# An attention and expert layer on one core: the order of far scores, maximum parts and the gated product within a pass of the loop

## The reference

```python
OFFSETS = sorted(set(range(0, 33)) | {48, 64, 96, 128, 192, 256, 384})
qkv = x @ Wqkv + bqkv                      # x: (16, 512, 256)
scores = stack([einsum('bhnd,bhnd->bhn', q, shift(k, d)) for d in OFFSETS]) * scale + pos_bias
alpha = softmax(where(invalid, -inf, scores))
flat = sum_i alpha[..., i] * shift(v, OFFSETS[i])
x = layernorm(x + (flat * sigmoid(x @ Wgate + bgate)) @ Wout + bout)
logits = relu(x @ rw1 + rb1) @ rw2 + rb2   # 8 experts, top 2, at most 1024 rows each
y = sum over the two experts of prob * (relu(row @ ew1 + eb1) @ ew2 + eb2)
out = layernorm(x + y)
```

## Time and profile before

| | |
|---|---|
| median of 3 timed runs | 2030.01 us (2027.12 to 2035.88) |
| the profiled execution's own time | 2021.59 us |
| its span, first to last instruction | 2019.9 us |
| PE busy | 1514.6 us, 75% |
| DVE busy | 988.9 us, 49% |
| ACT busy | 905.3 us, 45% |
| POOL busy | 705.7 us, 35% |
| mean granted TensorE clock | 0.796 of full speed |

### The profile page before, as it was taken

The page is one execution under the profiler, slowest core; times in us unless marked ns, Lnnn a source line. Parts: engine busy times, 40 slices in busy tenths (PEclk is TensorE's granted clock), DMA queues, the critical chain, the costliest instruction groups (busy, mean ns, idle before and its releaser), DMA issues. The chain is left out here.

```text
span 2019.9 us, 72320 instructions
## 1 busy us (share of the span) xinstructions
PE 1514.6 (75%) x31232; PEld 1005.1 (50%) x31232; DVE 988.9 (49%) x2117; ACT 905.3 (45%) x1544; POOL 705.7 (35%) x654
## 2 busy tenths in 40 slices
PE   0555787877787787878777887878765499999980
PEld 0234455555454555445554555545553266676660
DVE  4213445554545554555545544564644355555525
ACT  1231443635354453535444453544433365655626
POOL 4221313525333342525333342534323113323335
PEclk9765777868787777868787777868876699999995
DMA  2464624345352524335342524335220333443428
GB/s 77 74 171 156 134 56 98 98 77 125 80 114 79 108 73 93 97 70 115 85 98 75 105 70 88 91 78 110 58 57 14 108 105 85 95 114 85 74 28 337
DMA packets 220103, 194.55 MB, mean 96 GB/s; under 512 B 66847, under 2 KB 207151, under 8 KB 219648
## 3 DMA queue, kind: packets, MB, share of 16 engines
q1 hardware_dynamic: 204464, 175.11, 35.0%
q0 software_dynamic: 15360, 15.10, 4.7%
HBM read 98.07 MB, written 86.18 MB: 91 GB/s over the span
## 5 line engine op out<-in xcount | busy, mean ns | idle before, releaser
L394 POOL TENSOR_TENSOR p<-p 128x512 f16<-128x512 f32 x96 | 129.3, 1347 | 434.3 <-ACT p L794 434.2
L808 ACT COPY featT<-gp 128x1024 f16<-128x1024 f16 x96 | 93.3, 1031 | 329.3 <-PE gp L539 329.3
L394 DVE TENSOR_TENSOR p<-p 128x512 f16<-128x512 f32 x96 | 94.3, 982 | 288.0 <-ACT p L794 287.5
L546 PE MATMUL gp<-featT,wr 128*128 128x512 f16 x768 | 198.8, 416 | 24.2 <-DVE mT L957 15.4
L1105 POOL DMA_INDIRECT disp<-y,sidx x128 | 175.7, 1372 | 53.5 <-issue 37.9
L1359 POOL DMA_INDIRECT xln<-y,place x64 | 104.9, 1640 | 216.4 <-DVE y L1501 175.9
L1397 PE MATMUL up<-rowsT,w 128*128 128x512 f16 x768 | 170.1, 381 | 10.3 <-DVE w L1474 5.3
L1411 PE MATMUL dn<-w,h 128*128 128x256 f16 x1536 | 170.1, 273 | 0.0
L621 PE MATMUL o<-v_near,p 128*32 128x66 f16 x2048 | 134.6, 204 | 40.6 <-issue 29.1
L793 ACT ACTIVATE p<-st 128x512 f16<-128x512 f32 x192 | 116.6, 607 | 102.7 <-PE st L590 98.7
L1411 PEld LDWEIGHTS dn<-w,h 128*128 128x128 f16 x1536 | 149.7, 98 | 17.3
(11 more groups left out here) (176 smaller groups left out, 3138.1 us busy)
## 6 DMA issues: line engine op xcount, KB each, us to landing
qk_dram<-qk SPq DMA_DIRECT2D x64, 256.0 KB, 2.5
v_near<-vs SPq DMA_DIRECT2D x224, 66.0 KB
qs<-qk_dram SPq DMA_DIRECT2D x96, 128.0 KB, 4.6
ks<-qk_dram SPq DMA_DIRECT2D x96, 128.0 KB, 7.4
o_dram<-o_far SPq DMA_DIRECT2D x64, 136.0 KB, 5.7
o_back<-o_dram SPq DMA_DIRECT2D x16, 544.0 KB, 3.9
v_dram<-vs SPq DMA_DIRECT2D x16, 528.0 KB
v_far<-v_dram SPq DMA_DIRECT2D x64, 132.0 KB
```

The source lines that it names most:

```text
L394: engine.tensor_tensor(p16[:, b, 1, :], p32[:, b, :], p16[:, b, 0, :], ALU.subtract).then_inc(is_split, 1)
L546: last = nc.tensor.matmul(dst, lhs(a, c), rhs(b, c), start=(k == 0), stop=(k == len(todo) - 1))
L808: gp_done(nc.scalar.copy(featT[:, i, :, :].rearrange("f c t -> f (c t)"), bank[:, :].bitcast(F16)), n, stage, PART_OF_T[stage], i)
```

## The change

It changes three tables and nothing that an instruction computes.

- The second pair of far scores moves from slot 0 to slot 1, behind `qk0`, and its exponentials and subtractions move from slots 1 and 2 to slots 2 and 3.
- In slots 6 and 7 `near0` and `near1` stand ahead of `w` and `y`, where they stood behind.
- `near3`, `far0`, `far1` and `t` of the maximum stage move one slot later each. Slot 8 then holds `near2` alone; in slot 10 `far0` stands ahead of the router's transposes, in slot 11 `far1` ahead of `h0`, and `t` ahead of `h1` in slot 12.

```diff
@@ SLOTS_OF @@
-    6: [("outp", "w"), ("maxp", "near0")],
-    7: [("outp", "y"), ("maxp", "near1")], 8: [("maxp", "near2"), ("maxp", "near3")],
-    9: [("maxp", "far0")], 10: [("maxp", "far1"), ("rout", "t"), ("split", "x")],
-    11: [("maxp", "t"), ("rout", "h0"), ("rank", "s0"), ("rank", "s1")],
-    12: [("rout", "h1"), ("gate0", "den0"), ("gate0", "inv0")], 13: [("rout", "h2"), ("rank", "s2"), ("rank", "s3")], 14: [("rout", "h3")], 15: [("feat", "x")],
+    6: [("maxp", "near0"), ("outp", "w")], 7: [("maxp", "near1"), ("outp", "y")], 8: [("maxp", "near2")],
+    9: [("maxp", "near3")], 10: [("maxp", "far0"), ("rout", "t"), ("split", "x")],
+    11: [("maxp", "far1"), ("rout", "h0"), ("rank", "s0"), ("rank", "s1")],
+    12: [("maxp", "t"), ("rout", "h1"), ("gate0", "den0"), ("gate0", "inv0")], 13: [("rout", "h2"), ("rank", "s2"), ("rank", "s3")],
+    14: [("rout", "h3")], 15: [("feat", "x")],
@@ @@
-SCORES_AT = [-1, 0, 4, 7, 10, 12]
-EXP_AT = [0, 1, 5, 8, 11, 13]
-SPLIT_AT = [1, 2, 6, 9, 12, 14]
+SCORES_AT = [-1, 1, 4, 7, 10, 12]
+EXP_AT = [0, 2, 5, 8, 11, 13]
+SPLIT_AT = [1, 3, 6, 9, 12, 14]
```

## The result

The changed kernel took 2040.39 us (median of 19 runs, 2027.59 to 2050.77), the kernel before 2025.86 us (19 runs, 2019.50 to 2036.58) beside it. The ratio is 1.0065, with a 95% interval of 1.0049 to 1.0080. So it is slower by 0.65%, where I had forecast 1.7% faster, with slower at 0.13. The profiled execution took 2046.25 us, more than its median, and that of the kernel before (2021.59) took less than its own: the two traces lie 24.7 us apart, the medians 14.5.

A forecast was written before the change was run, and what follows sets the result against it. TensorE, busy 75% of the span, was taken as the bound through its waits. 29 us from 14 passes, 4 at the start and 2 for the clock gave 35: 1986.6 us profiled, 1995 median, range 1960 to 2036.

The forecast's parts named there:

- my sum: Gain per attention-loop pass: 0.5 us in one sample pass, 3.7 in the one before it, mean 2.1.
- Part 1: Second far scores behind first projection: direct gain 1.1 and 1.9 us a pass; ks lands 3.7 and 4.5 us earlier.
- Part 2: near0 ahead of the gated product: product ends 2.9 or 0.1 us later, near3 starts 11.6 us after it.
- Rival 2: Maximum stage: near2's reduction stays pinned to residual, stall before near0 costs 1 us more; 2026 to 2030 us, chance 0.15.
- Part 3: Maximum stage, one part to a slot, mT later: waits before near3, far0 and for mT go; 3.4 or 3.8 us gained.
- 19.7 remain: From near2's start to h1: 24.5 us, less three waits and near2 itself, leaves 19.7 us.
- pass B: Sample pass of the kernel before, one of two alternating kinds; x transposes end at 926.18; forecast gain 0.5 us.
- rival 4: Stall before near0 puts gated product and following work at 1.2 GHz, costing 14 to 20 us; 2009 to 2015, chance 0.13.
- my 35: Whole kernel: total forecast gain of 35 us, 29 from 14 passes, 4 at the start, 2 for the clock.
- Rival 3: Loads of ks land no earlier, so near0 holds TensorE; 2.0 us a pass more, 2058 us, chance 0.12.
- 17.1 and 19.1: Times in us from POOL's last projection subtraction to the last ks landing, in two sample passes, assumed unchanged.

The follow-up runs named there:

- 5: The whole change run again, against the kernel before, on a chip where that takes 1978 us: 1963.82 us, ratio 0.9915.
- 7: Far scores behind qk0, one part to a slot, near1 ahead of y, w still ahead of near0, against the kernel before: 1944.98 us, ratio 0.9830.
- 13: Only the far scores moved behind qk0, against the kernel before, on a chip where that takes 2028 us: 2001.54 us, ratio 0.9874.
- 16: Far scores behind qk0 and near1 ahead of y, maximum stage otherwise as before, against the kernel before: 1988.65 us, ratio 0.9785.
- 15: Far scores behind qk0, y a slot later on ACT and two on DVE, old maximum stage, against the kernel before: 1986.14 us, ratio 0.9765.
- `y` late: Far scores behind qk0, one part to a slot, y a slot later on ACT and two on DVE, against the kernel before: 1943.36 us, ratio 0.9815.
- 9: The changed kernel once more, against the kernel before, on a chip where that takes 2028 us: 2039.55 us, ratio 1.0048.
- 10: The changed kernel with row scatters two slots later (first half) and one later (second half); ratio against the kernel before: 2064.61 us, 1.0156.
- near1 first: Far scores behind qk0, one part to a slot, near1 ahead of y, y late on ACT and DVE, against the kernel before: 2016.82 us, ratio 0.9925.

## Why the prediction was wrong

The table holds mean us of a pass over twelve passes, worked out from TensorE's timeline. A stage counts from its start to the start of the next; the wait that stands before a stage is put to that stage, and the waits inside the maximum stage and for mT have rows of their own.

| stage | before | changed | before, chip without gaps | changed, same chip |
|---|---|---|---|---|
| transposes, projection, second far scores | 14.3 | 12.6 | 13.8 | 13.5 |
| near0 and gated product, with the 0.64 before the first near value product that went | 10.6 | 11.3 | 10.4 | 11.6 |
| waits for reductions inside the maximum stage | 5.7 | 5.6 | 5.7 | 5.6 |
| h0 | 3.9 | 4.7 | 3.6 | 4.6 |
| fourth near scores | 1.7 | 4.1 | 1.7 | 1.6 |
| wait for mT | 1.2 | 0 | 1.5 | 0 |
| h1 | 2.8 | 4.2 | 3.1 | 2.7 |
| third value product | 3.9 | 1.6 | 1.6 | 1.6 |
| h2 and h3 | 6.1 | 5.3 | 5.3 | 5.3 |
| fourth value product, first far scores | 4.1 | 6.1 | 4.3 | 4.4 |
| all other stages | 36.4 | 36.1 | 36.7 | 35.8 |
| pass | 90.5 | 91.7 | 87.6 | 86.7 |

The first three rows and that for mT are what my sum was made of. They gave 2.3 us a pass on the chip of the result, where I had 2.1. The rows from h0 on that I had left as they were cost 3.7.

**Part 1 was right.** The wait ahead of the projection is 1.21 in the pass shown, 1.9 in the mean where the two waits before made 3.5: a gain of 1.6, forecast 1.1 and 1.9. POOL's last subtraction of the projection came 12.8 us after the transposes of x (forecast 12 to 13). In three measurements on two chips the part by itself is worth 1.0 to 1.3%.

**Part 2 was nearly right, and its price was hidden in the sum.** near0 and the copies' wait together stand 4.9 us a pass (58.7 / 12) where 3.3 and 1.75 were forecast. near3 started 979.29 - 968.43 = 10.9 after the product's end; I had said 11.6. But what it buys is nothing: in the table the waits for reductions stay at 5.6, only moved for the most part onto near3 (4.87 in the pass shown). The reduction that it waits for stands behind the residual, as I had worked out. Rival 2 had no gain for this reason, but its own sign, near3 more than 13 us after the product, did not come. The two swaps of this part pull apart: near0 ahead of the product costs 0.9% (experiments 5 and 7), while near1 ahead of `y` alone, with near0 left behind the product, took 14.5 us of these waits off twelve passes (experiments 13 and 16, on two chips). Moving the residual instead took 29.6 (13 and 15). Neither has a wait on ks in those twelve passes.

**Part 3 was the step that failed:** "19.7 remain", that is, from near3's start to h1 without waits every duration was taken as in the kernel before. In the changed kernel it is 1002.69 - 979.29 = 23.4. The waits went as forecast: none for mT, and none before far0 (0.88 in pass B). But the fourth near scores took 5.03 (997.11 to 1002.14) in place of 1.7, and h0 4.5 (992.59 to 997.11) in place of 3.5; in the table it is 0.8 and 1.1 us longer a pass. Then h1, the first product behind the gaps, took 4.41 where I had 2.76. The sum from the fourth near scores to the first far scores is 18.5 before and 21.4 after, 2.8 more (table, its wait for mT apart); on the chip without gaps it is 15.9 and 15.5, 0.4 less. So in these stages the kernel before lost 2.6 us a pass to being on a chip with gaps, the changed one 5.8. All of its passes together differ by 2.9 and 5.0 between the two chips, so 0.3 and -0.8 us lie elsewhere.

These are the granted clocks of the changed kernel (length, busy per engine, PEclk, DMA share, GB/s), over the gaps and over h1 behind them, and then h1 in the kernel whose scatters come later and in the changed kernel on the chip without gaps:
```profile
997.11:1002.00 4.89, 2.60 (x71) 1.70 (x70) 1.07 (x2) 1.27 (x2) 3.30 (x4) 1.00 0.11 33
1002.69:1007.10 4.41, 4.41 (x17) 1.55 (x16) 4.23 (x4) 1.27 (x2) 0.00 (x0) 0.62 0.01 4
```
```profile
1016.52:1019.28 2.76, 2.76 (x16) 1.16 (x15) 2.62 (x3) 1.25 (x2) 0.00 (x0) 1.00 0.00 0
```
```profile
968.78:971.54 2.76, 2.76 (x16) 1.16 (x15) 2.62 (x3) 1.25 (x2) 2.46 (x2) 1.00 0.11 32
```
The clock was at its 2.4 GHz level (granted 1.00) in the gaps and at 1.2 GHz for part of h1 behind them (0.62 in the mean), so part of the bill for the gaps comes in the next product: 4.41 against 2.76 us for the same twelve matmuls. It is no matter of one pass: h1 took 3.6 to 5.2 us in each of the twelve passes of the changed kernel, and 2.8 in each of the twelve of the same kernel on the chip without gaps and of the kernel with later scatters. A slow h1 is not always due to gaps, though: in the kernel before on the chip without them it took 4.3 to 4.5 us in three passes of twelve. That is rival 4's effect, from another cause. I had looked for it behind the stall before near0, and there the gated product got shorter, not longer (62.3 to 58.4 us over twelve passes): it ran at a mean granted clock of 0.52 in the kernel before and of 0.56 in the changed one, so there was hardly a faster clock to lose. The section of the Trainium skill that the prediction quotes (TensorE: Matmul & The Clock Gate, "HAM oscillation — how this bites in real kernels") has waits for DMAs as the cause. Here five gaps of 0.37 to 0.52 us with no named releaser stood before the fall.

**The sign** comes from these together: a gain of 1.0 to 1.3% from Part 1, a loss of about 0.9% by near0's place, of which near1 ahead of `y` gives some back (0.9785 against 0.9874, experiments 16 and 13), and the slots, which are worth 0 (1.0006) without gaps and cost 1.3% (1.0127) with them. Three chips out of five in the experiments have the gaps, and so have the traces of the result: the kernel before shows 26.4 us of them in the value products. These were in my own trace as "issue", between 0.2 and 0.5 us at a time in pass B, and I read past them. They were the sign that TensorE's order and POOL's scatter collide, and that a slot's shift changes what is hit. Behind the third value product stand h2 and h3, which took 0.8 us a pass longer with the gaps before them (6.1 against 5.3); behind the fourth near scores stands h1, which took 1.5 longer (4.2 against 2.7). Without gaps the change gains 0.85%, or 17 us, half of my 35. There the projection's rows gave 0.3 us a pass in place of 1.5 (the end of the loop, below), h0 took 1.1 more, and the other stages gave 0.9 back.

**Rival 3** (late ks, 2058) did not happen: ks landed 961.50 - 942.75 = 18.7 after POOL's last subtraction, between the 17.1 and 19.1 used.

**What stays open.** That these gaps follow POOL's indirect scatters is shown by moving them, and all traces agree. Of TensorE's "issue" gaps between 280 and 1400 us, those that end beside a scatter or up to 1.5 us behind it sum to 22 to 62 us in every trace from a chip with gaps, and to 0.3 to 6.8 us in every other. Why TensorE stands still during a scatter, and why on some chips only, is not shown. The DMA engines' share was 0.11 in the gaps of the pass shown, so they were not full there; but no run here changes how instructions reach TensorE. Nor is every "issue" gap one of these: `y` late, on a chip without them, has 10.5 us before near scores far from any scatter, most of it in single gaps of 1.0 to 1.7 us, and their cause is not known. That h1 is slow because of the gaps rests on the comparison of two kernels on one chip (the changed one and that with later scatters, experiments 9 and 10) and of one kernel on two, which agree. Why h0 is 0.8 to 1.1 us longer was not tested; its granted clock fell from 0.74 to 0.61 in the mean of the twelve passes, and the stretch ahead of it (985.55 to 992.59 in the pass shown) had 0.50.

## What to carry to other kernels

Do not pass over "issue" idle between small matmuls: find what the other engines do in that stretch, and if it recurs beside the same instruction, count what will lie beside it after a shift, and allow for a slower clock in the first large product behind it. Before moving a part ahead of a product to free a later engine, ask whether the late work can be moved instead: `y` late, with near0 behind the product, gave 0.9815 against 0.9915 for the whole change on one chip, and with near1 first 0.9925 against 1.0048 on another. Measure on more than one chip when a change is worth under 2%: the same edit was 0.85% faster on one and 0.65% slower on another.

## What the runs showed that I had not expected

- The same kernel took 1978 and 1981 us on two chips and 2028, 2028 and 2032 on three, 2.5% apart. The first have about half the gaps in the value products (11.7 against 24.8, 25.8 and 26.4 us over twelve passes), and none of theirs beside a scatter.
- The first wait behind the transposes of x is not steady, and the profile puts nearly all of it down to "issue" (21.3 and 32.4 us over twelve passes in the first two traces of the changed kernel). In every other pass the projection starts 0.1 us after ACT's copies end, 1.1 to 1.6 us behind the transposes, as forecast. In five of the six passes between it starts 1.3 to 5.2 us after them. The body of the loop holds two passes and ends just there, so its end is the likely reason; no run tests it. It took most of Part 1's direct gain on the chip without gaps:
```profile
L546 PE MATMUL gp<-featT,wqk 128*128 128x512 f16 x288 | 88.1, 470 | 33.6 <-issue 32.4 <-ACT featT L808 1.2
```
